# Head sums of an attention layer drained by ScalarE and weighed by GpSimd, and a part of VectorE's list work moved from the merge stages to the threshold chain

## What is computed

```
dots = einsum('bhid,bhjd->bhij', q, k) * SCALE
dots = einsum('bhij,hk->bkij', dots, pre_proj)
dots = where(causal, -inf, dots)
thresh = top_k(dots, 64)[0][..., -1:]
dots = where(dots < thresh, -inf, dots)
attn = softmax(dots, axis=-1)
out = einsum('bhij,bhjd->bhid', attn, v)       # values of the 16 heads
return out.reshape(b, n, H * DH) @ Wo + bo     # summed over the heads
```

## Time and profile before

| | |
|---|---|
| median of the runs shown | 2923.88 us |
| profiled execution, its own time | 2921.19 us |
| its span | 2919.2 us |
| granted TensorE clock, mean over the span | 0.88 of full speed |
| VectorE busy | 2416.2 us (83%) |
| TensorE busy (matmul) | 2267.3 us (78%) |
| ScalarE busy | 1397.5 us (48%) |
| GpSimd busy | 5.2 us |

### The profile page before, as it was taken

The page is one execution under the profiler, slowest core; times in us unless marked ns, Lnnn a source line. Parts: engine busy times, 40 slices in busy tenths (PEclk is TensorE's granted clock), DMA queues, the critical chain, the costliest instruction groups (busy, mean ns, idle before and its releaser), DMA issues.

```text
span 2919.2 us, 34402 instructions
## 1 busy us (share of the span) xinstructions
PE 2267.3 (78%) x10182; PEld 1327.0 (45%) x10182; DVE 2416.2 (83%) x9381; ACT 1397.5 (48%) x2143; POOL 5.2 (0%) x43
## 2 busy tenths in 40 slices
PE   6598556677677757778888889888994999874997
PEld 2554333334444424444444445455552555443664
DVE  2505599999999989999999999999998999984445
ACT  1121233344445535556566666666662676762221
POOL 0000000000000000000000000000000000000000
PEclk9699667777888878999999999999997999986998
DMA  2000000000000000000000000000000000001000
GB/s 61 1 1 1 1 1 1 1 1 1 1 1 1 1 0 1 1 1 1 1 1 1 1 1 1 1 1 1 1 1 1 1 1 1 1 1 51 1 1 15
DMA packets 15425, 11.52 MB, mean 4 GB/s; under 512 B 6892, under 2 KB 13686, under 8 KB 15222
## 3 DMA queue, kind: packets, MB, share of 16 engines
q1 hardware_dynamic: 11184, 6.82, 0.9%
q10 hardware_dynamic: 4038, 2.37, 0.3%
HBM read 8.14 MB, written 1.05 MB: 3 GB/s over the span
## 4 chain that ended last, share of the span: by engine, by line
DVE 69%; PE 21%; ACT 4%; issue 4%; DVEq 2%; ACTq 0%
DVE cand L1123 17%; DVE R L1172 10%; DVE r L1174 9%; DVE F L1193 5%; DVE W L1153 5%; DVE W L1152 4%; PE bank L920 4%; PE bank L840 3%; PE bank L928 2%; DVE WP L1187 2%; PE bank L808 2%; ACT R L555 1%; ACT R L548 1%; DVE W L1145 1%; DVE W L1146 1%
## 5 line engine op out<-in xcount | busy, mean ns | idle before, releaser
L808 PE MATMUL bank<-hT,qT 128*128 128x512 f32 (+3 forms) x1280 | 572.6, 585 | 239.7 <-ACT R L521 215.2
L840 PE MATMUL bank<-WP,Y 128*128 128x512 f32 x1088 | 630.7, 665 | 139.2 <-ACT WP L562 137.7
L1123 DVE MAX8 cand<-R 128x8 f32<-128x12 f32 (+15 forms) x4096 | 640.5, 224 | 7.7 <-ACT R L521 7.6
L562 ACT ACTIVATE WP<-bank 128x512 f32<-128x512 f32 x544 | 320.8, 593 | 400.4 <-PE bank L825 396.0
L824 PE MATMUL bank<-ident,R 128*128 128x128 f32 x2176 | 461.0, 294 | 14.7 <-ACT R L555 14.7
L808 PEld LDWEIGHTS bank<-hT,qT 128*128 128x128 f32 x1280 | 239.2, 206 | 489.1 <-ACT R L521 249.1
L825 PE MATMUL bank<-nidentb,F 128*128 128x128 bf16 x2176 | 428.4, 230 | 0.0
L555 ACT ACTIVATE R<-R,negm 128x144 f32<-128x144 f32 (+15 forms) x256 | 309.5, 1211 | 219.4 <-DVEq L1280 219.4
L548 ACT ACTIVATE R<-R,cutb 128x144 f32<-128x144 f32 (+15 forms) x256 | 309.9, 1211 | 210.7 <-DVEq L1165 209.1
L824 PEld LDWEIGHTS bank<-ident,R 128*128 128x128 f32 x2176 | 329.7, 152 | 158.2 <-issue 108.1
L521 ACT ACTIVATE R<-bank 128x1024 f32<-128x1024 f32 (+7 forms) x384 | 290.1, 773 | 166.7 <-PE bank L808 87.8
(11 more groups left out here) (230 smaller groups left out, 2121.4 us busy)
## 6 DMA issues: line engine op xcount, KB each, us to landing
R<-in_L_attn_Wkv ACTq DMA_DIRECT2D x2, 512.0 KB, 8.7
R<-in_L_ffn_gate_w SPq DMA_DIRECT2D x1, 1024.0 KB, 6.5
R<-in_L_ffn_up_w SPq DMA_DIRECT2D x1, 1024.0 KB, 9.4
out<-X SPq DMA_DIRECT2D x1, 1024.0 KB, 5.1
R<-in_L_attn_Wq ACTq DMA_DIRECT2D x1, 512.0 KB, 6.7
WP<-in_L_attn_Wo ACTq DMA_DIRECT2D x1, 512.0 KB, 10.5
R<-in_L_ffn_wi SPq DMA_DIRECT2D x1, 256.0 KB
R<-in_L_ffn_wo SPq DMA_DIRECT2D x1, 256.0 KB
```

Source lines behind the costliest of these rows:

```text
L808: last = pe.matmul(to, qT[:, k % 2, i, :], hT[:, a:b], start=True, stop=b < n, skip_group_check=True)
L840: pe.matmul(bank[6], Y[:, j, :], PT[:, (blocks_before(k) + j) % 4, :], start=(j == 0), stop=(j == k // 4))\
L1123: mark(dve.max(cand[:, :, c, i], lists(S[:, k % NS, i, 0:n], n, c)))
```

## The change

- ScalarE copies bank 7, all 512 columns, to SBUF when the head sums are there (`drain_heads`), after the late score drains of its step and ahead of the turns. The copy goes into Zs, whose content TensorE has read by then; `heads` is another name for it. `outputs(k)` on TensorE waits for that drain of group k-1 in place of VectorE's gather.
- VectorE's `gather_step` goes. `weigh_heads(p-2)`, after `memory_weights(p-1)`, waits for the drain and takes the reciprocal of the four weight sums.
- GpSimd multiplies the four heads by their reciprocals in place (508 columns), adds two and two (254), adds the two (127) and adds that to ACC (127), with a wait on its own semaphore after each.
- ScalarE's next drain into Zs (L571) waits for GpSimd's last add of the group before.
- In `pivots` each of the 16 stages issues three list instructions in place of four. The other 16, all of the next group's row i = 3, go into the chain of `threshold`: 3, 3, 3, 3 and 4 behind its five steps, where each step is then waited for by itself.
- At the end VectorE takes two reciprocals and waits for GpSimd's last add.

```diff
@@ tiles
+        heads = Zs[:, :].rearrange("p (i c) -> p i c", i=GU)
@@ GpSimd, behind its constants
+            pool.wait_ge(s_zero, 1)
+            for k in range(NG):
+                t, g = divmod(k, 4)
+                pool.wait_ge(s_rden, k + 1)
+                pool.tensor_tensor(heads[:, :, 0:P - 1], heads[:, :, 0:P - 1],
+                                   rden[:, :].unsqueeze(2).to_broadcast([P, GU, P - 1]), ALU.mult).then_inc(s_sum, 1)
+                pool.wait_ge(s_sum, 3 * k + 1)
+                pool.tensor_tensor(heads[:, 0:2, 0:P - 1], heads[:, 0:2, 0:P - 1], heads[:, 2:4, 0:P - 1], ALU.add)\
+                    .then_inc(s_sum, 1)
+                pool.wait_ge(s_sum, 3 * k + 2)
+                pool.tensor_tensor(heads[:, 0, 0:P - 1], heads[:, 0, 0:P - 1], heads[:, 1, 0:P - 1], ALU.add)\
+                    .then_inc(s_sum, 1)
+                pool.wait_ge(s_sum, 3 * k + 3)
+                pool.tensor_tensor(ACC[:, t, 0:P - 1], heads[:, 0, 0:P - 1], bob[:, 0:P - 1] if g == 0 else ACC[:, t, 0:P - 1],
+                                   ALU.add).then_inc(s_acc, 1)
+                pool.wait_ge(s_acc, k + 1)
@@ ScalarE
+            def drain_heads(k):
+                act.wait_ge(s_yb, k + 1)
+                act.activation(Zs[:, :], bank[7], ACT.Copy).then_inc(s_heads, 1)
...
                 act.wait_ge(s_pv, blocks_before(k + 1))
+                if k:
+                    act.wait_ge(s_acc, k)
                 act.activation(Zs[:, :], bank[6], ACT.Copy).then_inc(s_zs, 1)
...
                     drain_late(p + 1, GU)
+                    if p >= 2:
+                        drain_heads(p - 2)
                     for j in turns[0:3]:
...
+            drain_heads(NG - 1)
@@ TensorE, outputs
                 if k:
-                    pe.wait_ge(s_acc, k)
+                    pe.wait_ge(s_heads, k)
@@ VectorE, pivots
-                    list_step(k + 1, 4 * step, 4)
+                    list_step(k + 1, 3 * step, 3)
@@ VectorE
-            def gather_step(k, n):
...
+            def weigh_heads(k):
+                dve.wait_ge(s_heads, k + 1)
+                dve.reciprocal(rden[:, :], heads[:, :, P - 1]).then_inc(s_rden, 1)
@@ VectorE, threshold
+                def beside(ins, first, count):
+                    mark(ins)
+                    link_ = done[0]
+                    list_step(k + 1, 3 * CH + first, count)
+                    dve.wait_ge(s_dve, link_)
...
-                link(gather_step(k - 2, 0))
-                mark(dve.tensor_scalar(idx[:, :], idx[:, :], HALF, -HALF, ALU.add, ALU.add))
-                link(gather_step(k - 2, 1))
...
+                beside(dve.tensor_scalar(idx[:, :], cnt[:, k % 2, :], -0.5, TOPK - n / 2 + 0.25, ALU.mult, ALU.add), 0, 3)
+                beside(dve.tensor_scalar(idx[:, :], idx[:, :], HALF, -HALF, ALU.add, ALU.add), 3, 3)
+                beside(dve.tensor_tensor(hit[:, :, :], place[:, :].unsqueeze(1).to_broadcast([P, GU, 9]), bc(idx[:, :], 9),
+                                         ALU.is_equal), 6, 3)
+                beside(dve.tensor_tensor(hit[:, :, :], hit[:, :, :], r9[:, :, :], ALU.mult), 9, 3)
+                beside(dve.tensor_reduce(th, hit[:, :, :], AX.X, ALU.add), 12, 4)
@@ VectorE, the loop and its end
                 if p >= 1:
                     memory_weights(p - 1)
+                if p >= 2:
+                    weigh_heads(p - 2)
...
             for k in (NG - 2, NG - 1):
-                for n in range(5):
-                    link(gather_step(k, n))
-                dve.sem_inc(s_acc, 1)
+                weigh_heads(k)
+            dve.wait_ge(s_acc, NG)
```

More of the change, by code:

```diff
@@ L322, in build @@
         s_yb, s_acc = sem("s_yb"), sem("s_acc")
+        s_rden = sem("s_rden")
+        s_zero = sem("s_zero")
+        s_heads = sem("s_heads")
+        s_sum = sem("s_sum")
         s_y1 = sem("s_y1")
@@ L1110, in _ @@
             link(dve.memset(doubts[:, :, :], 0.0))
+            dve.sem_inc(s_zero, 1)
             def list_step(k, first, count):
@@ L1233, in threshold @@
                 dve.wait_ge(s_eight, GU * k + GU)
-                mark(dve.tensor_scalar(idx[:, :], cnt[:, k % 2, :], -0.5, TOPK - n / 2 + 0.25, ALU.mult, ALU.add))
+                def beside(ins, first, count):
[3 more added lines that the diff above has]
+                    dve.wait_ge(s_dve, link_)
                 mark(dve.scalar_tensor_tensor(out=tie[:, :], in0=r9[:, :, 1], scalar=-BIG_, in1=cutb[:, k % 2, :],
                                               op0=ALU.mult, op1=ALU.is_le))
-                link(gather_step(k - 2, 0))
-                mark(dve.tensor_scalar(idx[:, :], idx[:, :], HALF, -HALF, ALU.add, ALU.add))
-                link(gather_step(k - 2, 1))
[L1240 to L1250, removed]
+                beside(dve.tensor_scalar(idx[:, :], cnt[:, k % 2, :], -0.5, TOPK - n / 2 + 0.25, ALU.mult, ALU.add), 0, 3)
[4 more added lines that the diff above has]
+                beside(dve.tensor_reduce(th, hit[:, :, :], AX.X, ALU.add), 12, 4)
                 if t == 0:
```

## The result

The changed kernel takes 2824.2 us (median of 4 runs, 2821.21 to 2831.97) against 2923.65; the ratio is 0.9667, with a 95% interval of 0.9642 to 0.9692. On two later occasions, each beside fresh runs of the kernel before, the ratio was 0.9683 (0.9666 to 0.9701) and 0.9683 (0.9666 to 0.9700), 89 and 91 us between the medians.

A forecast was written before the change was run, and what follows sets the result against it. VectorE was taken as the bound, with TensorE and ScalarE as late in the last groups. Savings of 87.3 + 6 - 1.8 = 91.5 us, less 26.5 for collisions, gave 65.0 less: 2858.9 us, range 2828 to 2906.

The forecast's parts named there:

- The bound, and the chain: VectorE bounds most groups; taking the gather out of the threshold chain saves 1.72 us per group, 2.29 less 0.57.
- the reciprocal: In weigh_heads on VectorE: one reciprocal, now from SBUF, taken as 0.10 us per group, leaving 1.62 us.
- The move itself costs and gives nothing: Merge stages to threshold chain: the 16 moved lists cost 2.45 us in either place, so moving them is neutral.
- The collisions: At the four scans: GpSimd steps overhanging the MAX8 delay the next scan, 0.5 us average over 53 groups, 26.5 us.
- The last groups: Groups 55 to 63: TensorE and ScalarE are as late as VectorE, so they gain only 6 us.
- ScalarE's drains cost nothing before that: In the loop: the head-sum drain (0.6 us) fits ScalarE's idle gaps, so VectorE does not wait for it.
- The tail: After the last head sums: drain, reciprocal and GpSimd chain take 3.7 us instead of 1.9, adding 1.8 us.
- The sum: Whole kernel: 91.5 us saved less 26.5 for collisions, 65.0 us less, 2858.9 us on the median.
- no-collision case: Rival at the scans: VectorE and GpSimd do not hinder each other, 91.5 us less, 2832.4 us; chance 0.25.
- late-TensorE rival: TensorE becomes the bound from tile 10 on; groups 41 to 54 give nothing, 22.7 us lost, 2882 us; chance 0.08.
- the slower one: Rival at the scans: GpSimd's whole chain stands in VectorE's way, 2.9 us a group, 2986 us; chance 0.06.

## Why the prediction was off

*The bound, and the chain.* Right. 1.75 us a group against 1.72 (the step shares that I listed add up to 0.55, not 0.57, which makes it 1.74); the reciprocal 4.1 us over groups 2 to 54 against 5.3; groups 0 and 1 gave 0.72 and 0.74 (0.7).

*"The move itself costs and gives nothing."* Right as I used it, wrong as a description. The 16 lists cost the same in both places, but half of the gain, 44 us, comes with them alone: the 1.72 I gave to taking out the gather needs the lists to fill the gaps.

*The collisions.* This is the step that failed: "on average 0.5: 26.5 us". The mechanism is the forecast's, and in all but a few groups even the order is (the scan first, by 0.05 us), but over the same 53 groups the scans grew by 9.6 us, 0.18 each. Three sizes were off. The multiply is 1.03 us, not 1.35, and 0.89 when it has been queued. A scan is released 0.21 us before the GpSimd step ends. And the overhangs that I averaged by eye are a sawtooth over the tiles: 0.3 to 0.4 us a group in tiles 0 to 2, nothing in 4, 0.44 in 5, falling by 0.13 a tile to nothing in 9 and 10, 0.18 again in 11, while I had up to 1.5 in tile 0. The price of all four steps together, 2.9, was nearly right (2.65); that two-input steps are nearer to the dearer row was wrong for the step that matters.

*The last groups.* Groups 55 to 62 gave 7.9, 10.3 and 8.9 us in the three profiles, against 6. As forecast, the engines behind VectorE are late now: before the last tile's mask VectorE waits 4.46 us for TensorE, 3.64 before. In group 60 VectorE waits 0.85 us for ScalarE's drain, which has itself waited for TensorE (timelines of ScalarE and of VectorE):

```profile
2355.95 0.60 ACT L575 ACTIVATE Zs<-bank 128x512 f32<-128x512 f32 x1 [1.12 <-PE bank L892]
```

```profile
2356.58 0.18 DVE L1213 RECIPROCAL rden<-Zs 128x4 f32<-128x4 f32 x1 [0.85 <-ACT Zs L575]
```

*ScalarE's drains cost nothing before that.* Right. Group 39 of the changed kernel:

```profile
1440.97 0.60 ACT L575 ACTIVATE Zs<-bank 128x512 f32<-128x512 f32 x1 [0.67 <-PE bank L892]
1441.65 1.28 ACT L588 ACTIVATE WP<-bank 128x512 f32<-128x512 f32 x2
...
1447.32 1.38 ACT L570 ACTIVATE R<-R,cutb 128x1296 f32<-128x1296 f32 x1 [2.58 <-DVEq L1197]
```

The drain fell into the 1.35 us gap of the earlier trace rows, and the wait at the cut went from 5.00 to 2.58.

*The tail.* From the last head sums to L988 (L957 before) some 3.9 us instead of 1.9: +2.0 against +1.8. What follows, the unchanged last layer, took 261.8 us in the first profile of before and 259.2 in its second; in the changed kernel's three it took 259.2 to 259.3. That is scatter too.

*The sum.* The span of the first profile is 94.4 us shorter: 89.2 in the loop, 4.6 ahead of it and 2.6 in the last layer by scatter, less 2.0 in the tail. Of the loop I had 66.8 (87.3 + 6 - 26.5). The 22.4 between are 16.9 for the collisions, 1.3 in the chain, 1.2 for the reciprocal, 1.9 in the last groups and about 1 that single groups have elsewhere. The low end of the range was the no-collision case with 4 us for the late groups alone: it left no room for the scatter of single executions, which is 12 us for this kernel (2820.18 to 2831.97). The first median, 2824.2, fell below it, and the two later ones, 2829.7 and 2829.1, lie just inside: which side of the bound it is was chance, the missing 22 us in the loop were not. The times are nearest to the "no collision" rival's 2832.4, but that rival is wrong as a mechanism: the collisions are there, and small. The late-TensorE rival did not come (groups 41 to 54, which it had at nothing, gave 22.5 us), nor did the slower one.

## What to carry to other kernels

In a chain of short dependent steps, read what each step costs when waited for and when not: independent work placed in the gaps was worth about as much here (44 us) as taking the five head-sum instructions off the engine (48 us). Before elementwise work goes to GpSimd, look at what VectorE runs beside it: the scans here, which read two SBUF operands, and GpSimd steps that read SBUF kept each other out, so give such steps a place beside one-operand instructions, and send them early enough to be queued but not so early that they go first; a margin of 0.05 us was not safe. When a sum is to be right to a few us, compare a stretch of the kernel that repeats, not the end-to-end time.

## What the runs showed of the hardware

- The exclusion is per instruction and goes by order: 0.17 us of start time turned a delay of the GpSimd multiply by 1.4 us into a delay of the scan by 0.70.
- The recorded starts do not settle the order to 0.05 us: at a recorded 0.05 us behind the scan the multiply waited in 178 groups of three profiles and went first in 5.
- A held scan went on 0.20 to 0.21 us before the recorded end of the GpSimd step.
- The recorded length of a step includes its standing still: 2.41 us for a GpSimd multiply that takes 1.03, and 2.27 us for a scan that takes 1.57.
- The time at which the same code reached the loop scattered between 332.5 and 340.1 us over twelve profiles, in values that recur (332.5 to 333.2, 334.8, 336.8 to 337.9, 339.7 to 340.1).
